# Scan stage of a Mamba layer: B's rows for VectorE's inflows spread by DMA and copied to PSUM by ScalarE instead of one-hot products on TensorE

## The reference

```python
u, z = jnp.split(x @ in_w.T, 2, axis=-1)
u = silu(depthwise_conv4(u) + conv_b)
dbc = u @ xproj_w.T                      # dt rank 64, then B (16 rows), then C (16 rows)
dt = softplus(dbc[..., :64] @ dt_w.T + dt_b)
dA = exp(dt[..., None] * A)              # per token, channel and state n
dBu = (dt * u)[..., None] * B[:, :, None, :]
h = dA_t * h + dBu_t                     # over time
y = einsum('bdn,bn->bd', h, C_t)
out = (y + u * D) * silu(z) @ out_w.T
```

## Time and profile before

| | us |
|---|---|
| median of 3 runs | 1371.97 |
| lowest, highest | 1368.11, 1373.04 |
| span of the profiled execution | 1397.4 |
| scan stage in it, first to last scan | 42 to 804 |

### The profile page before, as it was taken

How to read it: one execution, slowest core, us unless ns; L and a number is a source line. 1 busy time by engine, 2 the same in 40 slices (tenths; PEclk the granted TensorE clock), 3 DMA queues, 4 the chain that set the end, 5 groups by cost and what they waited for, 6 DMA issues and landing times.

```text
span 1397.4 us, 27753 instructions
## 1 busy us (share of the span) xinstructions
PE 1272.1 (91%) x9894; PEld 962.1 (69%) x9894; DVE 1097.7 (79%) x1829; ACT 947.2 (68%) x1630; POOL 1013.4 (73%) x620
## 2 busy tenths in 40 slices
PE   6799999999999999999998779999989999986695
PEld 2567767676777676766766646689966666656693
DVE  5799999999999999999999953333357888874475
ACT  5888988898889888988988842245545555532243
POOL 2789999999999999999999916223334665664442
PEclk9999999999999999999999999999999999998798
DMA  5545434543444454444444351312152000021223
GB/s 187 145 131 161 138 139 118 161 149 129 139 139 165 133 150 139 164 132 152 139 146 111 114 216 47 90 44 86 56 157 86 2 1 1 13 64 34 79 72 100
DMA packets 153014, 154.73 MB, mean 111 GB/s; under 512 B 96624, under 2 KB 121712, under 8 KB 143168
## 3 DMA queue, kind: packets, MB, share of 16 engines
q1 hardware_dynamic: 148112, 143.16, 32.8%
q0 software_dynamic: 4768, 9.81, 2.2%
HBM read 138.66 MB, written 20.20 MB: 114 GB/s over the span
## 4 chain that ended last, share of the span: by engine, by line
PE 49%; ACT 21%; DVE 16%; issue 8%; another core or an unknown queue 2%; DMA 2%; POOL 1%; SPq 1%; DVEq 1%; POOLq 0%; ACTq 0%
DVE hh L887 7%; PE pq L410 6%; ACT da L720 6%; PE pa L506 4%; PE py L525 3%; ACT pa L725 3%; PE bank L1562 3%; PE bank L1558 2%; PE pr L2016 2%; PE bank L1572 2%; PE pr L2219 2%; PE pr L2030 2%; PE bank L1478 2%; DVE hh L897 2%
## 5 line engine op out<-in xcount | busy, mean ns | idle before, releaser
L1042 POOL TENSOR_TENSOR hc<-hh,cs 128x1024 f32<-128x1024 f32 x256 | 596.9, 2369 | 24.6 <-DVE hh L887 21.7
L887 DVE TENSOR_TENSOR_SCAN hh<-da,st,pa 128x512 f32<-128x512 f32 x240 | 292.7, 1261 | 14.1 <-PE pa L506 12.6
L525 PE MATMUL py<-ident,hc 128*128 128x128 f32 x2048 | 268.4, 277 | 7.4 <-ACT yt L738 5.8
L525 PEld LDWEIGHTS py<-ident,hc 128*128 128x128 f32 x2048 | 229.1, 141 | 54.4 <-issue 29.1
L506 PEld LDWEIGHTS pa<-dg,dtut 64*128 64x128 f32 x2560 | 160.9, 189 | 107.0 <-issue 103.2
L506 PE MATMUL pa<-dg,dtut 64*128 64x128 f32 x2560 | 189.8, 285 | 29.6 <-DVE hh L887 20.6
L720 ACT ACTIVATE da<-dt,w 128x512 f32<-128x512 f32 x320 | 209.7, 711 | 0.2
L897 DVE TENSOR_TENSOR_SCAN hh<-pa,st,hh 128x512 f32<-128x512 f32 x144 | 175.2, 1265 | 6.1 <-POOL hh L1032 3.7
L725 ACT ACTIVATE pa<-dt,w 128x512 f32<-128x512 f32 x192 | 124.5, 680 | 35.2 <-DVE hh L887 20.8
L410 PE MATMUL pq<-xn,w 128*128 128x512 f32 x248 | 124.6, 627 | 3.6 <-ACT xn L755 3.6
L1032 POOL TENSOR_TENSOR hh<-dtu,bs 128x1024 f32<-128x1024 f32 x48 | 112.8, 2365 | 3.1 <-issue 1.9
(11 more groups left out here) (341 smaller groups left out, 2643.8 us busy)
## 6 DMA issues: line engine op xcount, KB each, us to landing
cs<-bcrows SPq DMA_DIRECT2D x64, 1024.0 KB, 4.9
dg<-blocks SPq DMA_DIRECT2D x80, 256.0 KB, 5.0
bs<-bcrows SPq DMA_DIRECT2D x48, 256.0 KB, 3.7
blocks<-bcrows SPq DMA_DIRECT2D x320, 1.0 KB, 3.2
xsorted<-in_pads SPq DMA_DIRECT2D x13, 387.0 KB, 5.7
rot<-in_rot SPq DMA_DIRECT2D x4, 1024.0 KB, 4.9
wx<-in_l_w SPq DMA_DIRECT2D x4, 1024.0 KB, 10.0
ysort<-ytoken SPq DMA_DIRECT2D x14, 256.0 KB
```

The source lines that it names most:

```text
L525: i = pe.matmul(py[:, h * CH + kt * P:h * CH + (kt + 1) * P], hc[s % HCS][:, h, t], ident[:, :], is_transpose=True, start=n == 0 and kt == ...
L887: v.tensor_tensor_scan(hh[(NS * m + nj) % HHS][:, h, :], da[q % DAS][:, :], inflows, 0.0 if first else st[:, m % 2, nj, h:h + 1], ALU.mult ...
L1042: g.tensor_tensor(hc[s % HCS][:, :, :], hh[s % HHS][:, :, :], cs[j % 2][:, s % CG, :].unsqueeze(1).broadcast_to([P, HF, CH]), ALU.mult).th ...
```

## The change

The tile `sel` and its input go, and `spread_b` leaves TensorE's list. SyncE issues one DMA for each unit and each n of BY_V (`b_row_in`, 48 in all), which reads row n of B from DRAM and spreads it over the 128 partitions of one of four new tiles `brow`. ScalarE copies that tile to the bank `pb` (a new `spread_b`), at the ends of its steps 0, 5 and 11, behind `prep` and `keep_dtu`. ScalarE waits there for the DMA, for VectorE's last inflow (`s_db`) and for its own `keep_dtu`. `keep_rows` no longer waits for the products. The four semaphores `s_back`, used late in the program, are shared with the new DMAs, so that their later counts begin at `back0` (192), and each later wait on them is raised by as much.

```diff
+SPREAD_AT = (0, 5, 11)
-SLOTS, DAS, BG = 4, 4, 2
+SLOTS, DAS, BG, BVS = 4, 4, 2, 4
...
-                sel = sb(k, "sel", [P, NS])
+                brow = [sb(k, f"brow{i}", [P, CH]) for i in range(BVS)]
...
-                    def spread_b(s):
-                        m, n = s // NS, s % NS
-                        if made(BY_V, s) >= 2:
-                            pe.wait_ge(s_db, made(BY_V, s) - 1)
-                        pe.wait_ge(s_turnk, turned_count(m, HF - 1))
-                        pe.matmul(pb[:, :], sel[:, n:n + 1].broadcast_to([P, P]), crow[m % 2][:, :], start=True, stop=True).then_inc(s_b, 1)
...
-                        if s + 2 < STEPS and by_vector(s + 2):
-                            spread_b(s + 2)
...
                             act.wait_ge(s_cout, 16 * (m - 1))
-                            act.wait_ge(s_b, len(BY_V) * (m - 1))
...
+                    def spread_b(s):
+                        m = s // NS
+                        k = made(BY_V, s) - 1
+                        act.wait_ge(s_brow[k % BVS], 16 * (k // BVS + 1))
+                        if k >= 1:
+                            act.wait_ge(s_db, k)
+                        act.wait_ge(s_turnk, turned_count(m, HF - 1))
+                        act.activation(pb[:, :], brow[k % BVS][:, :], ACT.Identity).then_inc(s_b, 1)
...
                         prep(s // NS + 1, s % NS)
                         if s % NS == 0:
                             keep_dtu(s // NS, 1)
+                        if s % NS in SPREAD_AT:
+                            spread_b(s // NS * NS + BY_V[SPREAD_AT.index(s % NS)])
...
-                            sy.dma_start(sel[:, :], a["sel"]).then_inc(s_small, 16)
...
+                    def b_row_in(k):
+
+                        m = k // len(BY_V)
+                        sy.wait_ge(s_cout, 16 * (m + 1))
+                        if k >= BVS:
+                            sy.wait_ge(s_b, k - BVS + 1)
+                        sy.dma_start(brow[k % BVS][:, :], bcrows[m][BY_V[k % len(BY_V)], :].partition_broadcast(P)).then_inc(s_brow[k % BVS], 16)
...
                     load_block(0)
+                    for i in range(len(BY_V)):
+                        b_row_in(i)
...
                             b_in(m + 1, 0)
                             for i in range(2):
+                                b_row_in((m + 1) * len(BY_V) + i)
+                            for i in range(2):
                                 diagonals_out((m + 1) * len(PAIRS) + i)
                         c_in(4 * m + 3)
                         if m + 1 < UNITS:
+                            b_row_in((m + 1) * len(BY_V) + 2)
                             for i in range(2, len(PAIRS)):
```

More of the change, by code:

```diff
@@ L103, in build @@
         s_phase = sem("phase_done")
+        s_back = [sem(f"b_row_in_then_back_in{i}") for i in range(4)]
+        back0 = 16 * (UNITS * len(BY_V) // BVS)
         phases = [0]
@@ L214, in layer0_mamba @@
             s_dtu = sem("dtu_made")
-            s_b, s_db, s_gdb = sem("b_spread"), sem("inflow_by_vector"), sem("inflow_by_gpsimd")
+            s_b, s_db, s_gdb = sem("b_rows_in_psum"), sem("inflow_by_vector"), sem("inflow_by_gpsimd")
+            s_brow = s_back
             s_pin = sem("inflow_by_tensor")
@@ L558, in mamba_tensor @@
                     pe.wait_ge(s_xv, 2)
-                    pe.wait_ge(s_small, 80)
+                    pe.wait_ge(s_small, 64)
                     pe.wait_ge(s_slot, slot_count(turn["relu", 0, HF - 1]))
@@ L769, in mamba_scalar @@
                     roots(range(0, 4), 1)
-                    act.wait_ge(s_small, 80)
+                    act.wait_ge(s_small, 64)
                     keep_turned(0)
@@ L976, in mamba_vector @@
                     rows(2)
-                    v.wait_ge(s_small, 80)
+                    v.wait_ge(s_small, 64)
                     keep_turned(1)
@@ L1050, in mamba_gpsimd @@
                         count["ng"] += 4
-                    g.wait_ge(s_small, 80)
+                    g.wait_ge(s_small, 64)
                     inflow(0)
@@ L1190, in build @@
         s_xsort, s_scat, s_ret = sem("sorted_in"), sem("scattered"), sem("returned")
-        s_back = [sem(f"back_in{i}") for i in range(4)]
         s_back0 = sem("first_back_in")
@@ L2109, in final_tensor @@
                     for q in (6, 7):
-                        pe.wait_ge(s_back[q % 4], 16 * B + 16 * (q // 4) + 16)
+                        pe.wait_ge(s_back[q % 4], back0 + 16 * B + 16 * (q // 4) + 16)
                         pe.matmul(summed(q), ident[:, :], back1[:, piece(q), :], start=False, stop=True).then_inc(s_yo, 1)
@@ L2116, in final_added @@
                     else:
-                        v.wait_ge(s_back[q % 4], 16 * B + 16 * (q // 4) + 16)
+                        v.wait_ge(s_back[q % 4], back0 + 16 * B + 16 * (q // 4) + 16)
                         v.tensor_tensor(bx[:, piece(q), :], x1[:, piece(q), :], back1[:, piece(q), :], ALU.add).then_inc(s_iadd, 1)
@@ L2538, in experts_in @@
                         else:
-                            v.wait_ge(s_back[chunks[0] // 4], 16 * B)
+                            v.wait_ge(s_back[chunks[0] // 4], back0 + 16 * B)
                         for t in tiles:
@@ L2821, in constants @@
     k["centre"] = np.eye(D, dtype=np.float32) - np.float32(1.0 / D)
-    k["sel"] = (np.arange(P)[:, None] == np.arange(NS)).astype(np.float32)
     k["before"] = np.triu(np.ones((P, P), np.float32), 1).astype(mybir.dt.np(BF16))
```

## The result

The changed kernel takes 1462.21 us (median of 5 runs, 1460.64 to 1469.46), the kernel before 1368.9 us (5 runs, 1364.98 to 1373.04): ratio 1.069, 95% interval 1.066 to 1.072. It is slower by 93 us; 74 were forecast, and the time lies 4 us above the range. The span of its profiled execution is 1467.3 us. Against the 1397.4 of the kernel before that is only 70 us more, because the one profiled execution of the kernel before lost some 25 us behind the scan stage: at the last reading of `pb`, the two stand at 887.26 and 792.45 us, 94.8 apart, and behind it at 580.0 and 604.9 (577.9 in experiment 6, whose code there is the same). The scan stage holds the whole difference.

What follows compares the result with a forecast made beforehand. Two loops through VectorE, GpSimd, TensorE and ScalarE were taken to bound the 47.69 us unit. 14 x (3.5 + 0.3 + 1.2) = 70, plus 2 (unit 14) and 1.5 (unit 0), gave 74: 1446 us, range 1424 to 1458.

Steps and rivals of the forecast that it cites:

- Two loops, and zero gain from the products: Loop A and loop B set the 47.69 us unit; removing TensorE's one-hot products, 2.9 us a unit, gains nothing.
- loop A: GpSimd waits 1.09 us a unit for VectorE's scan, then works without a gap to step 7's inflow, which VectorE awaits.
- loop B: TensorE waits 0.48 us for VectorE's scans, runs through step 14's inflow to the turned `dtu`; ScalarE's decays then release VectorE.
- The third copy: At ScalarE's step 11, behind relu_again and keep_pre: stalls VectorE's reading 3.5 us in units 0 to 13, 1.9 in unit 14.
- The wait that it brings: TensorE waits 3.3 us for softplus_sum ahead of the inflow of step 14, where there was no wait.
- The clock term: TensorE's clock falls behind its new wait at step 14's inflow: 1.2 us a unit on average, bounds 0 and 1.7.
- The copy at step 0: ScalarE's copy ahead of `da`, `silu` and step 4's decays: 0.54 less 0.1 and 0.15, net 0.3 us a unit.
- Step 5, SyncE: ScalarE's copy at step 5 is hidden ahead of a 0.84 us wait; the 48 DMAs are hidden in units 1 to 15.
- Unit 0: Three DMA issues of about 0.4 us go ahead of the diagonals TensorE waits for: 1.5 us, between 0 and 3.
- More than forecast: Rival: rows land late or the clock falls again at step 4; another 1 us a unit, 1460 us; chance 0.07.
- The stall alone, at full clock: Rival: VectorE's stall comes but TensorE's clock doesn't fall; 1429 us; chance 0.20.
- Faster: Rival: TensorE's 2.9 us a unit were the bound, so GpSimd's 1.09 us wait goes; 16 us, 1356 us; chance 0.03.

Runs made afterwards that it cites:

- experiment 6: Changed kernel with row 4 again by TensorE's product and rows 10 and 13 copied at the ends of ScalarE's steps 5 and 10: 1374.05 us, ratio 1.003.
- experiment 9: Kernel before with GpSimd's inflow of step 7 made one product earlier, nothing else changed: 1367.67 us, ratio 0.998.
- experiment 3: Changed kernel with rows 4 and 10 again by TensorE's products, row 13 alone copied at step 11, all 48 DMAs kept: 1439.85 us, ratio 1.052.
- Experiment 2: Changed kernel with three more, repeated passes on TensorE at its step 12, in its wait for softplus_sum: 1434.42 us, ratio 1.048.
- experiment 4: Changed kernel with row 13 alone copied at step 11 and three repeated TensorE passes in the wait that follows: 1423.1 us, ratio 1.040.
- experiment 1: Changed kernel with its third copy at the end of ScalarE's step 10 instead of step 11: 1383.14 us, ratio 1.011.
- experiment 7: No copies or products: VectorE's inflow reads the spread row in SBUF where the DMA put it: 1418.11 us, ratio 1.037 to the kernel before.

## Why the prediction was right and where it was wrong

- **Two loops, and zero gain from the products: right.** Experiment 6 shows it for the units, experiment 9 that loop A alone isn't the bound. The kernels with both loops shortened gain 0.5 to 0.9 us a unit. That loop A binds too is read from the trace before, where it closes without a gap; no kernel shortened loop B alone.
- **The third copy: right.** Forecast 3.5 us, measured 3.43; 1.9 forecast for unit 14, where the stall is 1.71.
- **The wait that it brings: right.** 3.3 us forecast, 3.33 measured. GpSimd's wait is 6.33 us instead of the 4.5 that I named: GpSimd stands idle for whatever makes the unit longer, the clock's part too (6.33 and a second wait of 1.74, less the 1.09 of before, are the 7.0 us by which the unit grew).
- **The clock term failed.** I wrote "That costs 1.7 us at most" and took 1.2. The bound came from one wait in the trace before, behind which the clock had been low for 3.4 us; the two other low stretches of that stage, from 57.1 and from 797.8 us, were 3.4 us long as well. Here it was low for 6.8 us behind ten of the 14 waits (loss 3.4 us, 2.8 of it on the loop), for 3.4 behind three and not at all behind one. The length of the low stretches seen so far was no bound for the next. The Trainium skill ("TensorE: Matmul & The Clock Gate", "HAM oscillation — how this bites in real kernels"), cited there, had the direction: the clock fell behind the wait in 13 of these 14 units, though only in eight of 14 in experiment 3. Over the scan stage the term is what the others leave of 94.8: 94.8 - 49.8 (stalls) - 10.8 (step 0) - 0.9 (start) = 33 us, where 17 had been forecast. Experiment 2, which takes the low clock away, gives 33 in the profiled executions and 28 between the medians.
- **The copy at step 0 was undersized.** Forecast 0.3 us, measured 0.71 to 0.75. Neither of the two reliefs that I had subtracted was there to have (0.04 of the 0.15; none of the 0.1), and the copy's wait for ScalarE's own semaphore, 0.21 us, wasn't in the sum. 6 us in all.
- **Step 5, SyncE: right.** Nothing for either in a unit (experiment 6 keeps the copy and all 48 DMAs, at 47.70 us a unit).
- **Unit 0: open.** 0.9 us by the first reading, where 1.5 was forecast (83.38 - 3.43 against the 79.10 of the kernel before), but by luck: the stage started 3.0 us earlier in that execution and then took 3.8 us more to the reading, stall aside. By the other traces (experiment 6) the DMAs may cost from nothing to some us there.
- **Where the number fell.** Above 1458 us stood the rival "More than forecast", with a chance of 0.07, and neither of its mechanisms came: no copy waits for a DMA in the full units, and in units 0 to 12 the clock never falls but behind the wait of the forecast. The time was there for another reason.
- **The short rivals.** "The stall alone, at full clock", 51.5 a unit, is what single units and experiment 4 show (51.1 without the copy at step 0). "Faster" had its decisive point rightly placed, but its price wrong: with the copy in time (experiment 1) nothing is gained.

## What to carry to other kernels

Where an operation moves to another engine, its price is the place in that engine's list, not its duration: read, for each instruction that it is put behind, when the wait of that instruction ends, against the time at which the result is wanted. Where a new stall makes TensorE wait (here for 3.2 to 3.3 us), look at the granted clock behind the waits that the trace already has, and don't take the length of the low stretches seen there as the most that can come; filling the wait with repeated passes shows in one run what it costs. Before relieving a busy engine, close the loops that set the period, and check that the relieved work stands on one.

## What the runs showed of the hardware

The same wait of TensorE, 3.33 us, is followed by a low clock in some units and not in others of one execution (2.08 and 1.16 us for the same sixteen matmuls, experiment 3), and the low stretch behind it lasts 3.4 or 6.8 us. It can repeat either way: the changed kernel ran six units of 54.5 to 54.8 us in a row, each with the low clock at the same place, and experiment 3 four of 51.0 to 51.1 in a row with none. What decides it isn't shown. VectorE and GpSimd slow each other when VectorE's product of f32 has both operands in SBUF (1.20 us to 2.1 in the median, 3.3 at worst), and not when one operand is in PSUM. The Trainium skill ("GPSIMD Engine Reference", "Specifications") names contention of the two engines with two inputs in SBUF; experiment 7 agrees and gives the price. At step 0 ScalarE's copy starts 0.71 us behind the start of its own last instruction, for whose semaphore it waits, where the next instruction started 0.50 behind it before: 0.21 us, the same in units 1 to 15.
